# An attention block and a four-way selective scan on one core: square tiles, early residual, B and C rows ahead of the step, and another order on every engine

## Time and profile before

| | us |
|---|---|
| median of 3 runs (952.26 to 953.2) | 952.5 |
| the profiled execution | 952.36 |
| its span, first to last instruction | 950.5 |
| busy in it: PE, DVE, POOL, ACT | 846.2, 834.1, 819.5, 586.4 |
| mean granted clock of TensorE, share of 2.4 GHz | 0.947 |

### The profile page before, as it was taken

One profiled execution on the slowest core, in us unless ns is written; L12 is line 12 of the kernel. 1 busy time (PEld: TensorE's weight loads), 2 busy tenths in 40 slices (PEclk: granted clock), 3 DMA queues, 4 the chain that ended last, 5 costly groups with the idle time before them and its releaser, 6 DMA issues.

```text
span 950.5 us, 8874 instructions
## 1 busy us (share of the span) xinstructions
PE 846.2 (89%) x2178; PEld 362.0 (38%) x2178; DVE 834.1 (88%) x632; ACT 586.4 (62%) x798; POOL 819.5 (86%) x374
## 2 busy tenths in 40 slices
PE   5679989898998989899898998989899898989876
PEld 2234434343443434344343443434344343433322
DVE  2489999899998999989899899989999899989992
ACT  3575666658566584856758476665856657585341
POOL 0499999988989889898998999898898988989990
PEclk9799999899998999989998999989999899999997
DMA  1588888787777978779697888978878897887860
GB/s 47 193 325 282 311 264 332 257 309 272 273 296 252 336 261 305 277 254 333 240 328 252 294 284 270 331 251 312 271 284 288 257 334 263 305 274 275 324 251 3
DMA packets 78051, 258.35 MB, mean 272 GB/s; under 512 B 13104, under 2 KB 15408, under 8 KB 78000
## 3 DMA queue, kind: packets, MB, share of 16 engines
q1 hardware_dynamic: 78000, 257.79, 78.2%
HBM read 254.60 MB, written 3.15 MB: 271 GB/s over the span
## 4 chain that ended last, share of the span: by engine, by line
PE 47%; ACT 18%; issue 13%; DVE 11%; POOL 5%; DMA 4%; DVEq 0%; SPq 0%; POOLq 0%; ACTq 0%
PE ps_y L546 31%; ACT ps_x L730 5%; ACT L730 4%; DVE state L1027 3%; POOL inp L879 3%; PE ps_y L537 3%; PE ps_x L531 3%; DVE state L1041 2%; DMA c_all<-bc_dram 2%; DVE yg L1049 2%; DMA b_all<-bc_dram 2%; DVE ps_x L1017 2%; ACT L712 2%; POOL state L885 2%; PE ps_w L411 2%
## 5 line engine op out<-in xcount | busy, mean ns | idle before, releaser
L879 POOL TENSOR_TENSOR inp<-du,b_all 128x1024 f32<-128x1024 f32 x224 | 521.7, 2353 | 36.9 <-DVE ps_x L1034 25.8
L546 PE MATMUL ps_y<-state,packed 128*128 128x512 f32 x1024 | 496.1, 627 | 8.7 <-POOL state L885 7.2
L1034 DVE TENSOR_TENSOR_SCAN ps_x<-ps_x,inp 128x1024 f32<-128x1024 f32 x144 | 327.1, 2282 | 34.7 <-ACT ps_x L730 34.7
L730 ACT ACTIVATE ps_x<-step,a_neg 128x1024 f32<-128x1024 f32 x224 | 248.3, 1113 | 143.6 <-DVE state L1041 71.5
L546 PEld LDWEIGHTS ps_y<-state,packed 128*128 128x128 f32 x1024 | 202.6, 202 | 253.3 <-issue 234.6
L885 POOL TENSOR_TENSOR state<-state,c_all 128x1024 f32<-128x1024 f32 x112 | 261.9, 2351 | 42.9 <-DVE state L1027 42.9
L1034 DVE TENSOR_TENSOR_SCAN state<-ps_x,inp 128x1024 f32<-128x1024 f32 x80 | 180.5, 2273 | 2.5 <-ACT ps_x L730 1.5
L1041 DVE TENSOR_TENSOR state<-ps_x,c_all 128x1024 f32<-128x1024 f32 x144 | 172.0, 1213 | 1.2
L1027 DVE TENSOR_TENSOR_SCAN state<-decay,ps_x 128x1024 f32<-128x1024 f32 x32 | 72.8, 2276 | 2.8 <-ACT decay L737 2.7
L531 PE MATMUL ps_x<-u,w_b_wide 128*128 128x512 f32 x128 | 62.8, 614 | 4.5 <-DVE state L1041 4.5
L459 PE MATMUL ps_w<-xpad,w_conv 128*128 128x512 f32 x128 | 62.4, 611 | 3.3 <-ACT xpad L692 3.3
(11 more groups left out here) (116 smaller groups left out, 635.7 us busy)
## 6 DMA issues: line engine op xcount, KB each, us to landing
c_all<-bc_dram SPq DMA_DIRECT2D x256, 512.0 KB, 5.6
b_all<-bc_dram SPq DMA_DIRECT2D x224, 512.0 KB, 6.3
xt<-in_x_t SPq DMA_DIRECT2D x32, 64.0 KB, 4.9
bc_dram<-bc_rows SPq DMA_DIRECT2D x32, 64.0 KB, 1.7
out<-ofin SPq DMA_DIRECT2D x16, 64.0 KB, 6.3
packed<-in_packed SPq DMA_DIRECT2D x1, 635.0 KB, 4.1
packed<-in_packed SPq DMA_DIRECT2D x1, 129.0 KB, 2.4
w_qkv<-in_w_qkv SPq DMA_DIRECT2D x1, 64.0 KB, 2.0
```

The source lines that it names most:

```text
L546: last = mm(ps_y[:, HALF * half:HALF * (half + 1)], ident, state[n % H_RING][:, HALF * half:HALF * (half + 1)], start=(n == 0), stop=(n == ...
L730: f(ps_x[n % 2][:, :], step[b.buf][:, :], ACT.Exp, scale=a_neg[:, n:n + 1]).then_inc(ps_decay_done, 1)
L879: tt(inp[i % IN_RING][:, :], du[b.buf][:, :], b_all[i % B_RING][:, :], ALU.mult).then_inc(pool_inputs, 1)
L1034: v.tensor_tensor_scan(held if KIND[n] == "P" else x, x, inp[i % IN_RING][:, :], 0.0, ALU.mult, ALU.add).then_inc(scans, 1)
```

## The change

- **Square tiles.** `theta`, `pooled`, `gw`, `attn`, `attn_t`, `x2sq`, `osq` and `w_mean` get 128 partitions (or 128 columns), zeroed once where needed, and the matmuls that read them run over the full 128 x 128; `mean_w` takes the place of `mean_sq`.
- **Early residual.** The residual x2 is put into w1 by `hid_residual`, ahead of `hid_proj`, which now only adds.
- **B and C rows.** For all images but the first `bc_proj` writes w1, before `step_proj`, without waiting for the step; `bc_copy` comes before `softplus`; `step_proj`'s second half waits for `bc_copy`, and `qkv` and `out_square` wait for `step_done`. For the first image `bc_proj` keeps its bank and moves ahead of `step_proj`.
- **Tables.** `silu_table` and `exp_table` ask for the loads at their own places.
- **First images.** The attention of the second image moves ahead of the first image's conv; small matmuls on a zeroed tile (`warm`) stand between the first stages.
- **Order.** All five `steps` are reordered.

```diff
+            def warm(count):
+                for _ in range(count):
+                    mm(ps_x[0][:, 0:128], warm_zero[:, :], warm_zero[:, :], start=True, stop=True)
             def qkv(j):
...
-                    at_least(pe, bc_rows_done, j.num)
+                    at_least(pe, step_done, j.num)
             def step_proj(j, half):
                 pe.wait_ge(u_done, 2 * (j.num + 1))
                 if half == 0:
                     pe.wait_ge(gate_done, j.num + 1)
+                elif j.num > 0:
+                    pe.wait_ge(bc_rows_done, j.num + 1)
...
             def bc_proj(j):
                 pe.wait_ge(u_done, 2 * (j.num + 1))
-                if j.num > 0:
-                    pe.wait_ge(step_done, j.num + 1)
-                bank = ps_w if j.num > 0 else ps_y
+                bank = w1 if j.num > 0 else ps_y
...
+            def hid_residual(j):
+                if j.num < IMAGES - 1:
+                    pe.wait_ge(step_done, j.num + 2)
+                at_least(pe, ofin_done, j.num)
+                for rows in range(2):
+                    mm(w1[C * rows:C * (rows + 1), :], ident[:, C * rows:C * (rows + 1)],
+                       x2[j.num % X2_RING][:, :].unsqueeze(1).broadcast_to([128, 2, L]), start=True, stop=False)
             def hid_proj(j):
                 pe.wait_ge(yg_done, DIRS * (j.num + 1))
...
+                for d in range(DIRS):
+                    rows, e = d % 2, d // 2
+                    last = mm(w1[C * rows:C * (rows + 1), L * e:L * (e + 1)], w("w_out"), yg[:, d, :],
+                              start=False, stop=(e == 1))
...
-                mm(w1[0:C, 0:L], mean_w[0:C, 0:C], osq[:, :], start=True, stop=True).then_inc(oms_done, 1)
+                mm(w1[:, 0:L], mean_w[:, :], osq[:, :], start=True, stop=True).then_inc(oms_done, 1)
```

More of the change, by code:

```diff
@@ L348, in prologue @@
                 load_b(first, 7)
+                load_c(first, 3)
             def finish(j):
@@ L484, in bc_proj @@
                 last.then_inc(bc_mm, 1)
+            def hid_residual(j):
[5 more added lines that the diff above has]
+                       x2[j.num % X2_RING][:, :].unsqueeze(1).broadcast_to([128, 2, L]), start=True, stop=False)
             def hid_proj(j):
                 pe.wait_ge(yg_done, DIRS * (j.num + 1))
[L488 to L494, removed]
-                    last = mm(to, ident, x2[j.num % X2_RING][:, :], start=False, stop=True)
+                for d in range(DIRS):
+                    rows, e = d % 2, d // 2
+                    last = mm(w1[C * rows:C * (rows + 1), L * e:L * (e + 1)], w("w_out"), yg[:, d, :],
+                              start=False, stop=(e == 1))
                 last.then_inc(hid_mm, 1)
@@ L506, in out_mean @@
                 for e in range(2):
-                    last = mm(w1[0:C, 0:L], w_mean[:, :], hnorm[:, e, :], start=(e == 0), stop=(e == 1))
+                    last = mm(w1[:, 0:L], w_mean[:, :], hnorm[:, e, :], start=(e == 0), stop=(e == 1))
                 last.then_inc(ocen_mm, 1)
@@ L557, in prologue @@
                 step_weights()
+                warm(1)
                 attn_turn(first)
+                warm(1)
                 attn_out(first)
-                pe.wait_ge(zeroed, 10)
+                warm(2)
+                pe.wait_ge(zeroed, 9)
                 mean_square(first)
+                qkv(second)
+                warm(2)
+                scores(second)
+                warm(2)
                 pe.wait_ge(conv_weights_ready, 1)
@@ L564, in prologue @@
                 conv(first, 1)
+                attn_turn(second)
                 pe.wait_ge(weights_ready, 1)
                 gate_proj(first)
+                bc_proj(first)
                 step_proj(first, 1)
                 step_proj(first, 0)
-                bc_proj(first)
                 spread_b(first, 0)
-                qkv(second)
-                scores(second)
-                attn_turn(second)
                 attn_out(second)
             def finish(j):
+                sum_state(j, 14)
+                hid_residual(j)
                 sum_state(j, 13)
-                sum_state(j, 14)
                 sum_state(j, 15)
@@ L593, in steps @@
                 if done:
+                    hid_residual(done)
                     hid_proj(done)
@@ L896, in prologue @@
                 scan_input(first, 6)
-                scan_input(first, 7)
-                product(first, 3)
             def finish(j):
@@ L967, in setup @@
                 dve.wait_ge(wf4_done, 1)
-                v.tensor_scalar(w_mean[:, :], w("ident2"), -1.0 / C, wf4[:, :], ALU.add, ALU.mult)
+                for cols in range(2):
+                    v.tensor_scalar(w_mean[:, C * cols:C * (cols + 1)], w("ident2"), -1.0 / C, wf4[:, :], ALU.add, ALU.mult)
                 for k, n in enumerate(BY_DVE_IN):
@@ L1078, in prologue @@
                 attn_norm(second)
+                first_bc(first)
+                scan_input(first, 0)
             def finish(j):
-                product(j, 15)
                 gated(j)
```

206 lines of the change are left out of this document (110 added, 96 removed).

## The result

The changed kernel takes 901.3 us (median of 4 runs, 897.2 to 904.9) where the kernel before takes 952.5: 0.946 of it, 95% interval 0.942 to 0.950. The forecast was 903, its range 884 to 935. The profiled execution took 900.34 us with a span of 898.5, 1.84 us around it. In one experiment, the changed kernel without its three loads, one run of 948.4 us fell in a slower state of the chip and is left out of the time.

A forecast was written before the change was run, and what follows sets the result against it. No one engine is the bound; the period is DVE's 51.8 us plus waits. Scan 0 of image 1 at 87.5 + 13 x 53.3 + 52.0 + 69.0 = 901.4 us of span, forecast 903, range 884 to 935.

The forecast's parts named there:

- Tables: Explicit Exp loads on ACT: scan 7 waits 0.3 to 0.4 us for 1.75, scan 6 about 0.1 for 0.40.
- B and C rows: bc_proj ahead of step_proj: PE idle 1.3 us against 2.4; scan 9 and pooling cost 0.5, bounds 0 and 1.0.
- Padding: Small matmuls on PE widened: priced at 0; bounds 0.3 us gained and 1.3 us lost an image.
- Clock: TensorE's slow clock in a middle period: half of 1.2 us taken, from 52.7 to 53.3 us.
- Transfers: Loads in SP's new order: priced at 0, upper bound 1 us an image; shortest lead C row 2.
- First images: Prologue: scan 0 at 32 us, bounds 29 and 34; scan 0 of image 1 at 87.5 instead of 93.74.
- What was covered by nothing: residual before decay 1, out_squares before decay 6 on ACT: PE late by 1 us is DVE late by 1 us.
- rival (d): PE's lateness passes through ACT's queue at residual and out_squares: 58 us a period, 964 us; chance 0.13.
- (b): The clock falls as before for 6.9 us in each image: 54.8 us a period, 923 us; chance 0.20.
- (c): PE's cycle hardly shortens, sums wait for POOL's later products: 55.6 to 56.2 a period, 933 to 941 us; chance 0.11.
- Rival (a): POOL becomes the bound and the clock stays full: 52.0 us a period, 886 us; chance 0.14.
- The early hid_proj and the order of the last sums: End of the last image: sums about 1.5 us less, hid_proj 1.0 less; 69.0 us for 71.47.

The follow-up runs named there:

- the last experiment: The changed kernel with C rows issued sooner and POOL's product 10 ahead of input 13: 887.6 us, 0.932 of the kernel before.
- the one-load run: The kernel before with only an explicit Exp load behind gate_silu added: 904.2 us, 0.953 of the kernel before.

## Why the prediction was right, and where its terms were not

The sum held within 3 us: 898.5 of span for 901.4. Its parts, forecast and measured: image 1 begins 87.5 and 89.54; thirteen periods 692.9 and 686.8; image 14 52.0 and 52.48; last image 69.0 and 69.72. Errors of +2, -6 and +1 us add up to a good figure, in part by luck; the attribution was worse than the sum. In the middle period too, forecast at 52.7 us for full clock and measured at 52.83, two errors cancel: DVE's busy time, held at 51.8, is 51.25 to 51.45, and waits for C rows, priced at 0, cost 0.56 by the last experiment. And the forecast gave the gain to several edits, where one of them alone gives as much.

**Tables: mis-sized.** They were priced at the waits that end on them, scan 6 and scan 7, about 1.7 us an image. The waits came out near what was said (0.19 for 0.3 to 0.4 at scan 7; about 0.2 for 0.1 at scan 6, within its pair of 4.70 us), but the loads alone give 3.6 us an image. out_norm's 1.97 us and the slow clock were booked as terms of other edits (out_square's new place, bc_proj ahead); they hang on the same load, through softplus. In the one-load run gate_silu ends at 431.12 and the decay begins at 432.45, 1.33 us with the load of 1.28. The Trainium skill (ScalarE: Activation LUTs, What ACT_TABLE_LOAD costs) adds a drain of about 1.4 us to a load; this trace shows no room for one.

**B and C rows: the wait as said, the worth not.** PE waits 0.80 us there for a forecast of 1.3, softplus begins 27.4 us after scan 0 for 27.3. But once the load is early there is nothing left to gain: 901.3 with it, 902.4 without.

**Padding: priced at 0, bounds -0.3 to +1.3.** TensorE's time fell by 1.65 us an image, outside those bounds: I took a group's time to be set by the columns that stream, and padded groups, and unpadded ones beside them, got shorter all the same; why is open. In the new order the price on the path is 0 as forecast, within the intervals; in the order of before, without the loads, it was 21 us. The Trainium skill's rule that was weighed against this step (TensorEngine Tiling (Array Packing), The Solution: for small dimensions the array is reconfigured into independent tiles) gave 1.3 us more by the prediction's own estimate; these rows show the opposite sign for seven groups that have no partner to run beside.

**Clock: 0.6 us, measured 0.** No middle period has a fall, with PE's wait at 0.80 or in the loads alone at 0.47.

**Transfers: priced at 0, and the "shortest lead C row 2" was the wrong one.** Rows 4 and 14 are late. They are late by the new order of SP, which put them behind B rows; the order of before had them in time at the same period. C rows sooner give 0.56 us a period and 3.7 us in the first image; the bound of 1 us held for the middle.

**First images: scan 0 at 30.54 for 32 (bounds 29 to 34), but a first period of 59.0 for 55.5.** Most of the head start was lost again: in that period DVE waits 2.5 us for C rows, 2.3 ahead of pooling and 2.2 for an input from POOL, and POOL waits 3.4 for C rows and 1.3 for a B row. What the clock of 0.83 cost there was not separated. 3 us were allowed for this, 6.5 were needed.

**What was covered by nothing held.** residual ahead of decay 1 and out_squares ahead of decay 6 made no wait at scans 1 and 6; rival (d) is out. So are (b) and (c). Rival (a) was right that the clock stays full, and with C rows sooner the time is within 2 us of its 886. That POOL becomes the bound is not shown: in the period above POOL is busy 51.14 of 51.90 us and DVE 51.26. The early hid_proj and the order of the last sums, together 2.5 us at the end in the forecast, are worth about 5 there, and the early hid_proj half a us a period besides.

Open: the old order with the loads and the new first images stands at 898.2, and its middle period of 52.66 us is 0.4 above the mean of 52.27 that the new order has with C rows sooner. C rows sooner were not tried there. Nor was padding, though with the loads alone TensorE still has 46% of the chain. So what the new order itself is worth beyond the loads is not shown.

## What to carry to other kernels

A wait is not worth its own length: follow what is queued behind it until the cycle closes, and price all later waits that it feeds as one term. Before a reordering of five engines is tried, put an engine's table loads where it is idle. And when the engines' waits go, look at the order in the DMA queue next: rows that were in time in the old order of loads were late in the new one, at the same period of 53 us.

## What was not expected of the hardware

- Padded fp32 matmuls of 64 to 256 columns are not longer, and most are shorter: mean_square 0.59 us for 0.70, TensorE 48.29 for 49.94 us an image. An unpadded neighbour gained as much (0.59 for 0.70), so the time may lie in the step from one shape to another; no run here isolates it.
- The same wait of 2.14 us before bc_proj was followed by the low clock level in one period (1.73 us for bc_proj) and by the full one in the next (1.05), in turn, period by period. What decides between them is left open.
- The store of 64 KB of B and C rows takes 1.7 us to land in before, 2.4 with the loads alone and 6.3 in after. It takes 6.3 with SP's order of before in the changed kernel too, so that order is not the reason; the reason is left open.
